# Three of nine value taps made a group ahead by ScalarE and GpSimd; key maps built 13 columns wide

## The chip, the core and the metric

The kernel runs on one core of a Trainium2 chip. The metric is the device time of one execution in microseconds (us), smaller is better.

## The reference

The program is a residual network stage of two parts on x of shape (4, 128, 96, 96) in float32. The part that matters here is the first, an attention over channels:

```
kv = einsum('oc,bchw->bohw', qkv_w, gn(x));  kv = depthwise3x3(kv, qkv_conv_w);  k, v = split(kv)
q  = idwt2(depthwise3x3 of the four bands of dwt2(gn(x)))
q, k = q / |q|, k / |k|                      (over the 96x96 pixels, 8 heads of 16 channels)
attn = softmax(q k^T * temperature);  out = proj_w @ (attn v);  x = x + out
```

The second part is two binarized 3x3 convolutions with batch norms and a residual. The change touches how `v`'s depthwise 3x3 convolution (nine taps, "value taps") is computed, and how wide the blocks are in which the matrices for `k` ("key maps") are built.

## The kernel before

The program is four blocks one after the other: `block_stats_and_projections`, `block_grams`, `block_attention`, `block_convolutions`. The change lies in `block_grams`, which I call the gram stage.

The gram stage works through NG = 32 groups of GC = 4 channels, for all four images at once. Each group is a list of J = 20 jobs, written out in `SLOTS` in four pieces:

```
"u kg mq s1 tk",  "kg s1 mq u tk",  "kg s1 mq u tk",  "kg s1 mq u mq"
```

So job 0 is a `u`, 1 `kg`, 2 `mq`, 3 `s1`, 4 `tk`, 5 `kg`, 6 `s1`, 7 `mq`, 8 `u`, 9 `tk`, 10 `kg`, 11 `s1`, 12 `mq`, 13 `u`, 14 `tk`, 15 `kg`, 16 `s1`, 17 `mq`, 18 `u`, 19 `mq`. `s1` transforms a channel's rows, `u` applies its map matrices to the result of `s1` and makes the query feature (job 8 uses job 3, 13 uses 6, 18 uses 11, and job 0 of the next group uses 16), `kg` makes the key feature, `mq` and `tk` build the map matrices of the next group in up to three blocks of MT = 7 or KT = 14 columns.

Every job goes through three engines. TensorE (PE) sums it into one of NB = 5 PSUM banks, used in turn. ScalarE (ACT) waits for the sum (`s_pe`) and copies its high half to float16 in SBUF (L839). VectorE (DVE) waits for that (`s_hi`), subtracts and stores the low half (L892), and only then is the bank free (`s_dve`): TensorE begins job n only when VectorE is done with job n - 5, and a `u` only when VectorE is done with its `s1`. All engines take their work strictly in the order of the program.

Between the jobs there is other work, at places given by tables of job numbers:

- VectorE adds the value taps 1 to 8 of the group's slab (12 image rows; SLAB = 12) in two halves, 16 instructions a group at `TAP_AT` (L885). The running sum `vsum` lies in PSUM, and the last tap of a half writes `vacc` in SBUF.
- ScalarE begins each half with a seed, tap 0 written to `vsum` (L811, at jobs 1 and 11). For the next group it normalises x (L794, four instructions, ahead of job 4) and copies its high half (L801, ahead of job 13).
- GpSimd (POOL) subtracts to get x's low half (L678), spreads taps (L687), and once in four groups computes the null parts of a head (L699 to L715).
- SyncE waits for the group's last tap, stores `vacc` (L636), then loads the slab for the group after next into the same buffer of `vin` (L616).

Once in four groups a head (16 channels) is complete. Its gram is summed by TensorE during the following four groups: pieces of ten matmuls (L975) behind the job pieces, 4 of them in the first group of the four, 3 in the second (one behind its first job piece, two behind its third and fourth), 3 in the third (two behind its first and second job piece, one behind its third), and the small null matmuls in the fourth. ScalarE copies the halves out (L821): the first in the second group, behind job 5, the second in the third group, behind job 15.

Before group 0, `lead` builds the maps of group 0 in eight jobs, and the groups 4 to 27 run in a hardware loop of three turns of eight groups.

## Time and profile before

| | |
|---|---|
| median of 3 runs (lowest, highest) | 1455.79 us (1451.62, 1458.39) |
| the profiled execution: its own time, its span | 1448.98 us, 1447.1 us |
| busy in the span: PE, DVE, ACT, POOL | 1186.5, 1087.4, 806.6, 232.0 us |
| the gram stage | from about 190 us to about 940 us of the span |
| value taps L885 in it | 448 + 64 instructions of 128x576 |

The span runs from the first to the last instruction of the profiled execution, and its own time is 1.9 us longer. The profile gives the busy time of each engine, the time at which each instruction started, what an idle engine waited for, and the clock that TensorE was granted. A VectorE or ScalarE instruction's length overlaps a little with the next one's, so the rate at which they follow each other is read from start to start.

### The profile page before, as it was taken

How to read it: one execution, taken by the hardware profiler on the slowest of the kernel's cores; microseconds unless marked ns; L12 is line 12 of the kernel's file. 1: busy time of each engine (PE TensorE's matmuls, PEld its weight loads, DVE VectorE, ACT ScalarE, POOL GpSimd, SP SyncE). 2: the span in 40 equal slices, each digit the busy share in tenths (PEclk: the TensorE clock that was granted, in tenths of full speed). 3: DMA queues.
4: the chain of work that ended last, by engine and by line, in shares of the span. 5: the costliest groups of instructions: out<-in, count | busy, mean ns of one | idle time of the engine just before them, and what ended most of it. 6: DMA issues, size and time to landing. Idle time of an engine off the chain costs nothing. (4 is left out here: it accounts for less than half of the span.)

```text
span 1447.1 us, 35967 instructions
## 1 busy us (share of the span) xinstructions
PE 1186.5 (82%) x12644; PEld 926.0 (64%) x12644; DVE 1087.4 (75%) x1899; ACT 806.6 (56%) x1414; POOL 232.0 (16%) x241
## 2 busy tenths in 40 slices
PE   0999937889899898998989999725999998999900
PEld 0555537789899898988989898603555554555500
DVE  6677428999999899998999999445767654063394
ACT  0677745667767576675667666110442443866383
POOL 6100011131131311313213221102000010000000
PEclk9999958999999899999999999867899999999955
DMA  9976962534444345444444442067877430000069
GB/s 327 419 303 267 305 144 71 138 88 123 132 100 123 108 112 137 104 115 116 108 129 116 111 127 71 22 233 240 277 254 252 134 136 0 0 1 0 1 267 401
DMA packets 148700, 221.22 MB, mean 153 GB/s; under 512 B 115624, under 2 KB 116788, under 8 KB 144192
## 3 DMA queue, kind: packets, MB, share of 16 engines
q1 hardware_dynamic: 137456, 152.26, 34.8%
q0 software_dynamic: 6480, 47.19, 8.5%
q10 hardware_dynamic: 4608, 19.67, 4.0%
q8 instruction: 101, 1.65, 0.5%
q14 instruction: 55, 0.45, 0.1%
HBM read 131.84 MB, written 87.20 MB: 151 GB/s over the span
## 5 line engine op out<-in xcount | busy, mean ns | idle before, releaser
L885 DVE SCALAR_TENSOR_TENSOR b_value_sum<-b_vin,b_vtaps,b_value_sum 128x576 f32<-128x576 f32 x448 | 361.5, 807 | 2.4 <-ACT b_value_sum L811 2.0
L1608 PE MATMUL b_conv_bank<-b_sign,wsign 128*128 (+1 forms) x1728 | 296.8, 329 | 10.3 <-ACT b_sign L1388 7.7
L1608 PEld LDWEIGHTS b_conv_bank<-b_sign,wsign 128*128 128x128 bf16 x1728 | 168.7, 98 | 141.2 <-issue 29.0
L927 PE MATMUL b_bank<-b_yh,b_tmh 96*96 96x200 f16 x768 | 198.4, 258 | 53.5 <-DVE b_feat L892 23.6
L839 ACT CAST b_feat<-b_bank 96x400 f16<-96x400 f32 x255 | 124.9, 490 | 191.4 <-PE b_bank L929 188.0
L927 PE MATMUL b_bank<-b_tkh,b_kt 96*96 96x100 f16 x1536 | 224.5, 211 | 2.5 <-DVE b_tml L908 2.3
L929 PE MATMUL b_bank<-b_tkh,b_kt 96*96 96x100 f16 x1536 | 223.5, 211 | 0.0
L928 PE MATMUL b_bank<-b_tkl,b_kt 96*96 96x100 f16 x1536 | 223.4, 211 | 0.0
L927 PEld LDWEIGHTS b_bank<-b_tkh,b_kt 96*96 96x96 f16 x1536 | 194.9, 127 | 5.0 <-DVE b_tml L908 2.5
L929 PEld LDWEIGHTS b_bank<-b_tkh,b_kt 96*96 96x96 f16 x1536 | 195.1, 127 | 0.0
L929 PE MATMUL b_bank<-b_yh,b_tml 96*96 96x200 f16 x768 | 194.2, 253 | 0.0
L928 PE MATMUL b_bank<-b_yl,b_tmh 96*96 96x200 f16 x768 | 194.2, 253 | 0.0
L928 PEld LDWEIGHTS b_bank<-b_tkl,b_kt 96*96 96x96 f16 x1536 | 193.6, 126 | 0.0
L1407 ACT CAST b_y<-b_conv_bank 128x384 f32 (+1 forms) x192 | 91.3, 478 | 172.9 <-PE b_conv_bank L1608 170.9
L678 POOL TENSOR_TENSOR b_xl<-b_xraw,b_xh 96x1536 f16<-96x1536 f32 x32 | 99.4, 3106 | 506.1 <-ACT b_xh L801 506.1
L1493 DVE BATCH_NORM_STATS2 b_bny<-b_y (+1 forms) x192 | 103.3, 554 | 100.0 <-ACT b_y L1407 99.2
L892 DVE TENSOR_TENSOR b_feat<-b_bank,b_feat 96x400 f16<-96x400 f32 x256 | 143.2, 560 | 18.7 <-ACT b_feat L839 15.6
L927 PEld LDWEIGHTS b_bank<-b_yh,b_tmh 96*96 96x96 f16 x768 | 95.2, 124 | 74.6 <-DVE b_feat L892 38.9
L461 PE MATMUL b_pk<-b_x,b_w_image 128*128 128x384 f32 x384 | 131.2, 497 | 6.8 <-DVE b_khl L362 6.7
L461 PEld LDWEIGHTS b_pk<-b_x,b_w_image 128*128 128x128 f32 x384 | 72.2, 192 | 59.7 <-DVE b_khl L362 15.3
L975 PE MATMUL b_gram<-b_feat 96*128 96x256 f16 x800 | 101.8, 277 | 2.4 <-DVE b_feat L892 1.2
L839 ACT CAST b_tmh<-b_bank 96x504 f16<-96x504 f32 (+1 forms) x155 | 99.9, 644 | 0.0
(210 smaller groups left out, 2314.2 us busy)
## 6 DMA issues: line engine op xcount, KB each, us to landing
b_vin<-value_projection_scratch SPq DMA_DIRECT2D x32, 686.0 KB, 5.5
value_projection_scratch<-b_vout ACTq DMA_DIRECT2D x24, 784.0 KB, 4.6
keys_scratch<-b_khl SPq DMA_DIRECT2D x24, 784.0 KB, 3.5
b_kt<-keys_scratch SPq DMA_DIRECT2D x128, 147.0 KB, 3.0
b_xraw<-in_x SPq DMA_DIRECT2D x128, 144.0 KB, 5.0
values_scratch<-b_vacc SPq DMA_DIRECT2D x32, 576.0 KB, 3.2
b_values<-values_scratch SPq DMA_DIRECT2D x48, 384.0 KB, 3.7
out<-xs SPq DMA_DIRECT2D x25, 576.0 KB, 6.8
```

What stands on the lines that cost most here:

```text
L461: nc.tensor.matmul(psum_k[g % NBK][:, 0:CH], w_image[:, b % 2, v, :], x[:, b, at:at + CH], start=True, stop=True).then_inc(s_mm, 1)
L678: nc.gpsimd.tensor_tensor(xh[1][:, slot, :, :, :].rearrange("h b c w -> h (b c w)"), xraw[:, slot, :], xh[0][:, slot, :, :, :].rearrange(" ...
L839: nc.scalar.copy(*target(n, 0, k)).then_inc(s_hi, 1)
L885: nc.vector.scalar_tensor_tensor(whole if t == 8 else part, src, vtaps[:, t:t + 1], part, ALU.mult, ALU.add).then_inc(s_tap, 1)
L892: nc.vector.tensor_tensor(out, src, high, ALU.subtract).then_inc(s_dve, 1)
L927: nc.tensor.matmul(out, w_hi, m_hi, start=first, stop=False)
L928: nc.tensor.matmul(out, w_hi, m_lo, start=False, stop=False)
L929: return nc.tensor.matmul(out, w_lo, m_hi, start=False, stop=last)
L975: ins = nc.tensor.matmul(gbank[:, half:half + 4 * HD * RUN], f[:, 0:2 * HD * RUN], f, start=(blk == 0), stop=(blk == S2B // RUN - 1))
L1407: nc.scalar.copy(dst, cbank[k % NBK][:, 0:CH]).then_inc(s_y, 1)
L1493: V.bn_stats(bny[:, ds(r * RC + (b * NCH + k), 1), :].rearrange("p o s -> p (o s)"), y[:, b, ds(r * (RC * CH) + k * CH, CH)]).then_inc(s_b ...
L1608: ins = nc.tensor.matmul(cbank[k % NBK][:, 0:CH].rearrange("p (r c) -> p r c", c=W), p["wsign"][nth // NIMG][:, t * C:(t + 1) * C], padded ...
```

## The change

Taps 0, 1 and 2 of a slab are no longer made in the halves. ScalarE multiplies tap 0 into `vacc` and tap 1 into the new buffer `vprod` (two instructions over the whole slab, 128x1152), a group ahead, in front of job 7 (`PRODUCTS = 7`). GpSimd adds the two, multiplies tap 2 into `vprod` and adds it (three instructions over the slab). The seed is now a copy of that sum into `vsum`, and VectorE adds the six taps 3 to 8, 12 instructions a group. On ScalarE the four instructions that normalise x stand ahead of the jobs 0, 2, 3 and 4, and x's high half ahead of job 5. The second seed moves from job 11 to job 10. `vprod` shares its memory with the buffer of the null parts, so that ScalarE waits once a head for them (`s_edge`) and GpSimd for its own sums (`s_ptap`). The key maps are built in blocks of 13 columns; there are 8 blocks as before.

```diff
-KT, KPB = 14, 3
+KT, KPB = 13, 3
...
-        eprod = sb("b2_eprod", [W, 4, 2, NIMG * HD * 2])
+        vprod = sb("b2_products", [C, SLAB * W])
+        eprod = vprod[0:W, 0:8 * NIMG * HD * 2].rearrange("p (a s n) -> p a s n", a=4, s=2)
...
-        TAP_AT = (0, 1, 2, 3, 5, 6, 7, 8, 10, 11, 12, 13, 15, 16, 17, 18)
-        SEED_AT = (1, 11)
-        NORMALISE, HIGH_X = 4, 13
+        PSTEPS = 3
+        TAPS = (3, 4, 5, 6, 7, 8)
+        NTAP = 2 * len(TAPS)
+        TAP_AT = (1, 2, 3, 4, 6, 7, 11, 12, 13, 14, 16, 17)
+        SEED_AT = (1, 10)
+        NORMALISE_AT, HIGH_X, PRODUCTS = (0, 2, 3, 4), 5, 7
...
+            def value_products(i, slot):
+                acc = vacc[:, slot, :]
+                pool.wait_ge(s_tap0, i * 2 + 2)
+                nc.gpsimd.tensor_tensor(acc, acc, vprod[:], ALU.add).then_inc(s_ptap, 1)
+                pool.wait_ge(s_ptap, i * PSTEPS + 1)
+                nc.gpsimd.tensor_tensor(vprod[:].rearrange("p (r c) -> p r c", c=W),
+                                        vin[:, slot, :].rearrange("p (r c) -> p r c", c=WP)[:, 0:SLAB, 2:2 + W],
+                                        vtaps[:, 2:3].unsqueeze(2).broadcast_to([C, SLAB, W]), ALU.mult).then_inc(s_ptap, 1)
+                pool.wait_ge(s_ptap, i * PSTEPS + 2)
+                nc.gpsimd.tensor_tensor(acc, acc, vprod[:], ALU.add).then_inc(s_ptap, 1)
...
                     low_x(i + 1, (k + 1) % 2)
+                    value_products(i + 1, (k + 1) % 2)
...
+            def products(i, slot, loads):
+                act.wait_ge(s_vin[slot], loads * 16)
+                act.wait_ge(s_vst[slot], loads * 16)
+                if not isinstance(i, int) or i:
+                    act.wait_ge(s_ptap, i * PSTEPS)
+                for t, dst in ((0, vacc[:, slot, :]), (1, vprod[:])):
+                    nc.scalar.activation(dst.rearrange("p (r c) -> p r c", c=W),
+                                         vin[:, slot, :].rearrange("p (r c) -> p r c", c=WP)[:, 0:SLAB, t:t + W],
+                                         ACT.Copy, scale=vtaps[:, t:t + 1]).then_inc(s_tap0, 1)
...
                 if half == 0:
-                    act.wait_ge(s_vin[slot], loads * 16)
+                    act.wait_ge(s_ptap, i * PSTEPS + PSTEPS)
...
-                nc.scalar.activation(vsum[:, :, 0:HALF // 2 * W].rearrange("p b (r c) -> p b r c", c=W),
-                                     src.rearrange("p (b r) c -> p b r c", b=2),
-                                     ACT.Copy, scale=vtaps[:, 0:1]).then_inc(s_seed, 1)
+                nc.scalar.copy(vsum[:, :, 0:HALF // 2 * W],
+                               vacc[:, k % 2, half * HALF * W:(half + 1) * HALF * W].rearrange("p (b n) -> p b n", b=2)).then_inc(s_seed, 1)
...
+                    if n == PRODUCTS and how != LAST:
+                        if gram is not None and k % GPH == 1:
+                            act.wait_ge(s_edge, gram + 1)
+                        products(i + 1, (k + 1) % 2, pairs + ((k + 1) // 2 + 1))
...
-            normalise(0, 0, 1)
+            for im in range(NIMG):
+                normalise(0, 0, 1, im)
             high_x(0, 0)
+            products(0, 0, 1)
```

Three places of the order in which engines take their instructions. The first is ScalarE at the start of the gram stage. Before, the eight copies of the lead jobs (`b_tkh`, `b_tmh`) follow x's high half (`b_xh`):

```order
L794 ACTIVATE b_xraw<-b_xraw,row_stats 96x384 x3
L801 CAST b_xh<-b_xraw 96x1536 [waits b2_x_normalised]
L848 CAST b_tkh<-b_bank 96x3x12x14 [waits b2_job_summed] x2
L848 CAST b_tkh<-b_bank 96x2x12x14 [waits b2_job_summed]
L848 CAST b_tmh<-b_bank 96x3x24x7 [waits b2_job_summed] x4
L848 CAST b_tmh<-b_bank 96x2x24x7 [waits b2_job_summed]
L811 ACTIVATE b_value_sum<-b_vin,b_vtaps 128x2x288 [waits b2_value_slab_in0]
```

Now the two products of slab 0, and with them the wait for its load, stand in front of the lead copies:

```order
L820 ACTIVATE b_xraw<-b_xraw,row_stats 96x384 x3
L826 CAST b_xh<-b_xraw 96x1536 [waits b2_x_normalised]
L835 ACTIVATE b_vacc<-b_vin,b_vtaps 128x1152 [waits b2_value_slab_stored0,b2_value_slab_in0]
L835 ACTIVATE b_products<-b_vin,b_vtaps 128x1152
L887 CAST b_tkh<-b_bank 96x3x12x13 [waits b2_job_summed] x2
L887 CAST b_tkh<-b_bank 96x2x12x13 [waits b2_job_summed]
L887 CAST b_tmh<-b_bank 96x3x24x7 [waits b2_job_summed] x4
```

The wait for the slab has moved from behind the lead jobs to in front of them. The second place is ScalarE in a group of the gram stage. Before, from the seed ahead of job 1 to the copy of job 7:

```order
L811 ACTIVATE b_value_sum<-b_vin,b_vtaps 128x2x288 [waits b2_value_tap_added,b2_value_slab_in1]
L839 CAST b_feat<-b_bank 96x100x4 [waits b2_job_summed]
L839 CAST b_tmh<-b_bank 96x3x24x7 [waits b2_job_summed]
L839 CAST b_yh<-b_bank 96x8x50 [waits b2_job_summed]
L794 ACTIVATE b_xraw<-b_xraw,row_stats 96x384 [waits b2_x_rows_in0]
L794 ACTIVATE b_xraw<-b_xraw,row_stats 96x384 x3
L839 CAST b_tkh<-b_bank 96x3x12x14 [waits b2_job_summed]
L839 CAST b_feat<-b_bank 96x100x4 [waits b2_job_summed]
L839 CAST b_yh<-b_bank 96x8x50 [waits b2_job_summed]
L839 CAST b_tmh<-b_bank 96x3x24x7 [waits b2_job_summed]
```

The same group after the change, from the copy of job 2 to the copy of job 7:

```order
L876 CAST b_tmh<-b_bank 96x3x24x7 [waits b2_job_summed]
L820 ACTIVATE b_xraw<-b_xraw,row_stats 96x384
L876 CAST b_yh<-b_bank 96x8x50 [waits b2_job_summed]
L820 ACTIVATE b_xraw<-b_xraw,row_stats 96x384
L876 CAST b_tkh<-b_bank 96x3x12x13 [waits b2_job_summed]
L826 CAST b_xh<-b_xraw 96x1536 [waits b2_x_normalised]
L876 CAST b_feat<-b_bank 96x100x4 [waits b2_job_summed]
L876 CAST b_yh<-b_bank 96x8x50 [waits b2_job_summed]
L835 ACTIVATE b_vacc<-b_vin,b_vtaps 128x1152 [waits b2_value_products_added,b2_value_slab_stored0,b2_value_slab_in0]
L835 ACTIVATE b_products<-b_vin,b_vtaps 128x1152
L876 CAST b_tmh<-b_bank 96x3x24x7 [waits b2_job_summed]
```

Between the copies of the jobs 1 and 7 there stand now three of the four normalising instructions, x's high half and the two products; before there were the four normalising instructions alone. The third place is VectorE from job 7 on. Before, from the low half of job 7 (`b_tml`) to that of job 11 (`b_yl`):

```order
L892 TENSOR_TENSOR b_tml<-b_bank,b_tmh 96x3x24x7
L885 SCALAR_TENSOR_TENSOR b_value_sum<-b_vin,b_vtaps,b_value_sum 128x2x288
L892 TENSOR_TENSOR b_feat<-b_bank,b_feat 96x100x4
L885 SCALAR_TENSOR_TENSOR b_vacc<-b_vin,b_vtaps,b_value_sum 128x576
L892 TENSOR_TENSOR b_tkl<-b_bank,b_tkh 96x3x12x14
L892 TENSOR_TENSOR b_feat<-b_bank,b_feat 96x100x4
L885 SCALAR_TENSOR_TENSOR b_value_sum<-b_vin,b_vtaps,b_value_sum 128x2x288
L892 TENSOR_TENSOR b_yl<-b_bank,b_yh 96x8x50
```

After the change, the same stretch:

```order
L929 TENSOR_TENSOR b_tml<-b_bank,b_tmh 96x3x24x7
L922 SCALAR_TENSOR_TENSOR b_vacc<-b_vin,b_vtaps,b_value_sum 128x576
L929 TENSOR_TENSOR b_feat<-b_bank,b_feat 96x100x4
L929 TENSOR_TENSOR b_tkl<-b_bank,b_tkh 96x3x12x13
L929 TENSOR_TENSOR b_feat<-b_bank,b_feat 96x100x4
L929 TENSOR_TENSOR b_yl<-b_bank,b_yh 96x8x50
```

The half's last tap stands behind job 7 instead of job 8, and there are no taps behind the jobs 8, 9 and 10.

## Rows read from the trace of the kernel before

**Rows 1.** Windows: busy us and (instructions) of PE, PEld, DVE, ACT, POOL; clock, DMA.

```profile
500.00:600.00 100.00, 94.92 (x1482) 89.87 (x1481) 100.00 (x167) 68.08 (x128) 27.93 (x33) 1.00 0.48 124
```

**Rows 2.** Timeline, VectorE: start us, length us, instruction; two pieces of a group.

```profile
520.27 0.50 DVE L892 TENSOR_TENSOR b_tkl<-b_bank,b_tkh 96x336 f16<-96x336 f32 x1
520.69 0.56 DVE L892 TENSOR_TENSOR b_feat<-b_bank,b_feat 96x400 f16<-96x400 f32 x1
521.17 0.81 DVE L885 SCALAR_TENSOR_TENSOR b_value_sum<-b_vin,b_vtaps,b_value_sum 128x576 f32<-128x576 f32 x1
521.89 0.57 DVE L892 TENSOR_TENSOR b_yl<-b_bank,b_yh 96x400 f16<-96x400 f32 x1
...
523.10 0.68 DVE L892 TENSOR_TENSOR b_tml<-b_bank,b_tmh 96x504 f16<-96x504 f32 x1
523.69 0.81 DVE L885 SCALAR_TENSOR_TENSOR b_value_sum<-b_vin,b_vtaps,b_value_sum 128x576 f32<-128x576 f32 x1
...
524.90 0.80 DVE L885 SCALAR_TENSOR_TENSOR b_vacc<-b_vin,b_vtaps,b_value_sum 128x576 f32<-128x576 f32 x1
```

**Rows 3.** Timeline, TensorE: first matmul of each job, start us and length us.

```profile
522.53 0.27 PE L927 MATMUL b_bank<-b_yh,b_tmh 96*96 96x200 f16 x1
...
524.12 0.21 PE L927 MATMUL b_bank<-b_tkh,b_kt 96*96 96x100 f16 x1
...
525.75 0.38 PE L937 MATMUL b_bank<-b_rm,b_map_place 126*96 126x168 f16 x3
525.97 0.21 PE L927 MATMUL b_bank<-b_ana,b_xh 96*96 96x100 f16 x1
...
526.73 1.26 PE L975 MATMUL b_gram<-b_feat 96*128 96x256 f16 x10
527.83 0.21 PE L927 MATMUL b_bank<-b_tkh,b_kt 96*96 96x100 f16 x1
```

**Rows 4.** Timeline, ScalarE: a group from its first copy, start us and length us.

```profile
524.32 0.49 ACT L839 CAST b_feat<-b_bank 96x400 f16<-96x400 f32 x1 [1.93 <-PE b_bank L929]
...
526.42 0.48 ACT L839 CAST b_feat<-b_bank 96x400 f16<-96x400 f32 x1
526.80 0.68 ACT L839 CAST b_tmh<-b_bank 96x504 f16<-96x504 f32 x1
527.34 0.50 ACT L839 CAST b_yh<-b_bank 96x400 f16<-96x400 f32 x1
527.71 2.52 ACT L794 ACTIVATE b_xraw<-b_xraw,row_stats 96x384 f32<-96x384 f32 x4
530.12 0.60 ACT L839 CAST b_tkh<-b_bank 96x504 f16<-96x504 f32 x1
...
538.21 1.46 ACT L801 CAST b_xh<-b_xraw 96x1536 f16<-96x1536 f32 x1
539.58 0.49 ACT L839 CAST b_feat<-b_bank 96x400 f16<-96x400 f32 x1
...
546.05 0.49 ACT L839 CAST b_feat<-b_bank 96x400 f16<-96x400 f32 x1 [1.93 <-PE b_bank L929]
546.44 1.07 ACT L821 COPY b_gout<-b_gram 128x512 f32<-128x512 f32 x1
```

**Rows 5.** Groups by form, ScalarE: count, busy us, mean ns; the nearest row to a product.

```profile
L1209 ACT ACTIVATE wsign<-b_w1t 128x1152 bf16<-128x1152 f32 x1 | 1.1, 1146 | 0.0
```

**Rows 6.** Tile b_xl, GpSimd: duration ns min/median/max, first and last start.

```profile
L678 POOL TENSOR_TENSOR b_xl<-b_xraw,b_xh x32: 3096/3106/3115, 202.3 to 892.8; 96x1536 f16<-96x1536 f32 x32
```

**Rows 7.** Timeline, SyncE: issue of the slab load in the same group.

```profile
526.54 0.35 SPq L616 DMA_DIRECT2D b_vin<-value_projection_scratch  x1
```

**Rows 8.** Tile b_vin: time from the issue of its loads to landing.

```profile
DMA to landing us min/median/max: 4.7/5.5/8.1
```

**Rows 9.** Timeline, ScalarE, start of the stage: idle time in brackets.

```profile
202.14 1.39 ACT L848 CAST b_tkh<-b_bank 96x504 f16<-96x504 f32 x3
...
208.25 0.74 ACT L811 ACTIVATE b_value_sum<-b_vin,b_vtaps 128x576 f32<-128x576 f32 x1 [2.12 <-DMA b_vin<-value_projection_scratch]
```

More of the change, by code:

```diff
@@ L787, in _, with normalise @@
             act.wait_ge(s_c, 7 * 16)
-            def normalise(i, slot, loads):
-                act.wait_ge(s_xin[slot], loads * LOAD)
-                for im in range(NIMG):
-                    piece = xraw[:, slot, im * GC * W:(im + 1) * GC * W]
-                    last = nc.scalar.activation(piece, piece, ACT.Identity,
-                                                bias=p["row_stats"][0:H, ds(i + (NIMG * NG + im * NG), 1)],
-                                                scale=p["row_stats"][0:H, ds(i + im * NG, 1)])
-                last.then_inc(s_xn, 1)
+            def normalise(i, slot, loads, im):
+                if im == 0:
+                    act.wait_ge(s_xin[slot], loads * LOAD)
+                piece = xraw[:, slot, im * GC * W:(im + 1) * GC * W]
+                nc.scalar.activation(piece, piece, ACT.Identity,
+                                     bias=p["row_stats"][0:H, ds(i + (NIMG * NG + im * NG), 1)],
+                                     scale=p["row_stats"][0:H, ds(i + im * NG, 1)]).then_inc(s_xn, 1)
@@ L799, in high_x @@
             def high_x(i, slot):
-                act.wait_ge(s_xn, i + 1)
+                act.wait_ge(s_xn, i * NIMG + NIMG)
                 nc.scalar.copy(xh[0][:, slot, :, :, :].rearrange("h b c w -> h (b c w)"), xraw[:, slot, :]).then_inc(s_xh, 1)
-            def seed(k, i, half, loads):
-                slot = k % 2
+            def products(i, slot, loads):
[7 more added lines that the diff above has]
+                                         ACT.Copy, scale=vtaps[:, t:t + 1]).then_inc(s_tap0, 1)
@@ L869, in _, with tap @@
             dve.wait_ge(s_c, 7 * 16)
-            def tap(k, i, m, loads):
-                slot, half, t = k % 2, m // 8, m % 8 + 1
+            def tap(k, i, m):
+                slot, half, t = k % 2, m // len(TAPS), TAPS[m % len(TAPS)]
                 src = vin[:, slot, :].rearrange("p (r c) -> p r c", c=WP)[:, half * HALF + t // 3:(half + 1) * HALF + t // 3,
@@ L900, in body @@
                     if n in TAP_AT:
-                        tap(k, i, m, pairs + (k // 2 + 1))
+                        tap(k, i, m)
                         m += 1
-                assert m == 16, m
+                assert m == NTAP, m
             for m, (kind, j) in enumerate(lead):
```

29 lines of the change are left out of this document (18 added, 11 removed).

## The prediction

> **What bounds the kernel now.** I read the windows first, for which engine has no idle time in the gram stage. VectorE is busy for all of the 100 us, TensorE for 94.92, ScalarE for 68, GpSimd for 28, at full clock [rows 1]. The timeline of VectorE then gives what each of its instructions costs from start to start: a value tap 0.72 us, a low half of 400 columns 0.48, of 504 columns 0.59, of 336 columns 0.42 [rows 2]. A group has 16 taps, 12 low halves of 400 columns, six of 504 (four `mq`, two `tk`) and two of 336: 11.5 + 5.8 + 3.5 + 0.8 = 21.7 us. The first copies of two successive groups on ScalarE are 546.05 - 524.32 = 21.73 us apart [rows 4]. So a group takes just what VectorE needs, and VectorE is the bound.
>
> How far behind is TensorE? Its timeline gives a `u` 1.59 us, a `kg` 1.63, a build of three blocks 0.22, an `s1` 0.54, ten gram matmuls 1.10 [rows 3]. Four `u`, four `kg`, four `s1` and the 22 blocks are 6.4 + 6.5 + 2.2 + 1.6 = 16.7 us. With 4, 3, 3 and 0 gram pieces a group needs 21.1, 20.0, 20.0 and about 17.4 us (a bit under 1 us for the null matmuls, an estimate). TensorE alone would thus allow 19.6 us a group on average.
>
> **VectorE after the change.** Four taps fewer save 2.9 us. The `tk` halves shrink by 36 columns in 504, at 0.59 - 0.42 = 0.17 us for 168 columns 0.04 us each. VectorE then needs 18.7 to 18.8 us a group. If only totals counted, a group would take max(21.1, 18.8), 20.0, 20.0, 18.8, a mean of 20.0, and 32 groups would save some 55 us.
>
> **But ScalarE stands in the middle of each job.** A copy that comes late delays VectorE, and VectorE holds the bank of job n until TensorE wants it for job n + 5. So I walk through one group, from T, where ScalarE starts the copy of job 0. That is the end of TensorE's `u` (0.20 us past the start of the next job). Job 1, a `kg`, ends at T + 1.63 [rows 3, 4]. From there ScalarE has without a gap, in its new order: copy `kg` 0.38, normalise 0.60 (2.41 for four), copy `mq` 0.54, normalise 0.60, copy `s1` 0.37, normalise 0.60, copy `tk` 0.44 (0.60 long, less the overlap and the narrower block), x's high half 1.37, two copies 0.76, the products, and the copy of job 7 with its full length 0.68 [rows 4].
>
> A product is new. Its form is that of the old seed, 0.74 us for 576 elements [rows 9]. Between x's high half (1536 columns, 1.46) and a copy of 400 columns (0.49) an element costs 0.86 ns [rows 4], so 576 more make 1.24 us long, 1.17 from start to start. The lower bound is the row of 1152 elements without the scale from memory, 1146 ns [rows 5], about 1.07 from start to start; the upper one is twice a seed, 1.48 [rows 9]. I take 1.17, since form and length both lie between rows. The Trainium skill (ScalarE: Activation LUTs, section "What ACT_TABLE_LOAD costs") gives 280 ns + 0.833 ns an element for an ACTIVATE with one operand by pointer, an estimate of 1240 ns. By rows 5 alone each group's chain would be 0.2 us shorter.
>
> The sum is 6.34 without the two products and 8.68 with them: the copy of job 7 ends at T + 10.31. VectorE, idle by then, does low half 7 (0.59), the tap behind it (0.72), low half 8 (0.56 long): T + 12.2 with the handover. Only now may TensorE start job 13, which it could have reached at about T + 11.4 with two gram pieces in the way, and at T + 10.3 with one. Behind it in TensorE's queue are `u` 1.59, two blocks 0.15, `kg` 1.63, `s1` 0.54, three blocks 0.22, `u` 1.59, two blocks 0.15, the gram pieces of 1.10 each, and the next group's job 0, 1.59 + 0.20. That is 7.66 us and two, one or no gram pieces. On VectorE the low halves and taps from job 7 to job 16 take 9.1 us from T + 10.3, with 0.3 us in it for the seed at job 10, which must wait for the tap behind job 7; job 0 of the next group needs low half 16, so T' is not before 10.3 + 9.1 + 1.8 = T + 21.2. The four groups of a head give:
>
> - first (two pieces in the second half): 12.3 + 7.66 + 2.2 = 22.1 us;
> - second: the gram copy of 1.07 us [rows 4] stands ahead of job 7 too, so 23.1 to 23.2;
> - third: one piece, 21.0, so VectorE's 21.2;
> - fourth: 21.2.
>
> Together 87.7 us, where before there are 4 x 21.74 = 87.0. **The relief of VectorE is thus handed to ScalarE's order**: six full heads cost 6 x 0.7 = 4 us. The groups 0 to 3 have no gram pieces: 0.5 us saved each, 2 us. The last group has nothing to normalise or to multiply: it saves about 2 us of the 2.9. The first three of the last head together cost 1 us. At the four ends of a straight or looped stretch TensorE is done earlier by 0.5 us: 2 us saved. Sum of the stage: +4 - 2 - 2 + 1 - 2 = -1 us.
>
> **The start.** Before, the lead copies start at 202.14, and ScalarE waits for slab 0 only behind them, until 208.25 [rows 9]. Now slab 0's wait and its two products stand ahead: the lead copies start at 208.2 + 2.35 = 210.6, 8.4 us later. Queued behind are all lead copies, on VectorE their low halves, and TensorE's job 1. GpSimd's part of slab 0 hides in this: three times 1152 elements, 3.106 us for 1536 [rows 6] make 2.33 us each, done 7.4 us after the products at 218.0, while job 1's sum is ready at about 219. So +8.4 us, with 0.3 for the seed 8.7.
>
> **What else is costed at nothing.** GpSimd's 7.4 us a group lie between T + 9.6 and T + 17.1, and the seed wants them at T' + 0.4, so 4 us of cover; with the null parts (2304 elements, an estimate of 6 us from rows 6) it is done about 1.5 us into the next group, ahead of x's high half at 6.5 and the `s_edge` wait at 8. If GpSimd took over 11 us, the seed and all copies behind it would wait. The Trainium skill (GPSIMD Engine Reference, "8. Key points") says that GpSimd's SBUF interfaces are shared with VectorE, and that VectorE instructions with two SBUF inputs or in a two-port mode contend. The trace shows GpSimd at 3096 to 3115 ns in all 32 cases beside a full VectorE [rows 6]; VectorE's inputs there are one in PSUM and one in SBUF.
>
> The slab has less cover. Its load is issued after the last tap, 0.84 us behind that tap's end (524.90 + 0.80, then 526.54) [rows 2, 7], and lands 5.5 us later, at worst 8.1 [rows 8]. The last tap now ends 0.2 us after T' in a short group, so the slab is there at T' + 6.5, and the products want it at T' + 7.3.
>
> **Sum.** -1 + 8.7 = +7.7 us on the profiled execution's 1448.98, so 1456.7. That execution lies 6.8 us below the median of 1455.79; on the median I get 1463.5 us.
>
> **Rivals.**
>
> - *The relief arrives* (faster). If ScalarE's chain is no bound, for instance because its pieces run closer together than I add them, a group goes to 20.0 us: 1.7 x 28 = 48 us and 5 at the ends, less 8.7: 1411 us. For it: TensorE and VectorE have the totals. Against: each term of the chain is a row of the same instruction, and the chain would have to be 2 us shorter. Half a microsecond less in each group gives 14 us, 1449. The sign turns where the chain is 0.3 us shorter than my 8.68. 20% for all of this side beyond the half per cent.
> - *The slab comes late* (slower). If a load takes 8.1 us as the slowest did, the products wait 1.8 us at T' + 7.3, and everything behind them too: 28 groups, +50, 1513 us; if a third of the loads do, 1480. It decides from a landing time of 6.3 us on. 12%.
> - *VectorE and GpSimd slow each other.* GpSimd's busy time per group grows by 7.4 us; if a tenth of it were lost on either engine, 0.7 us a group or 22 in all, 1485. The unchanged 3106 ns speak against it, and by the skill's rule nothing contends. 3%.
> - *The start costs nothing*, if the slab lands earlier: 1455. The load is issued by the same queue at the same place, so 5%.
> - *My forecast*, chain-bound groups of 21.6 to 22.3 us on average: 1455 to 1475, 60%.
>
> **From these the chances.** The products' bounds move the chain by -0.2 to +0.6 us, 6 us down and 18 up over the stage. This measurement tells about half a per cent, 7.3 us, from no change, and my forecast lies just at this edge: slower by more than that 0.47, within it 0.32, faster 0.21. The range for eight times in ten goes from 1436, most of the way to the half-microsecond rival and beyond, to 1484.
>
> **What would show each step.** In the changed kernel's profile VectorE should have 12 taps a group and be idle some 2 us before low half 7, waiting for ScalarE; a product should be 1.24 us long; TensorE should wait for VectorE's `feat` low half ahead of job 13; successive groups should be 22.1, 23.2, 21.2, 21.2 us; the lead copies should start near 210.6, behind a wait for the slab's DMA. I am wrong if TensorE's waits in the stage shrink to nothing (then the first rival), or if the products wait for the slab in most groups (the second).

## The result, and the profile after

| | before | after |
|---|---|---|
| median of 11 runs (lowest, highest), us | 1455.79 (1447.56, 1458.39) | 1462.15 (1459.49, 1469.23) |
| the profiled execution: time, span, us | 1448.98, 1447.1 | 1467.67, 1466.0 |
| T of group 4, T of group 28, start of the last tap, us | 301.86, 833.77, 918.5 | 307.03, 852.21, 936.7 |

The ratio after/before is 1.0065, 95% interval 1.0043 to 1.0088: a little slower. The two profiled executions lie at the edges of their runs, one 6.8 us below its median and one 5.5 us above. They differ by 18.7 us where the medians differ by 6.4. So I read from the traces which terms there are, and from the medians how large the sum is.

The page of the changed kernel begins with the span and the busy times:

```profile
span 1466.0 us, 36146 instructions
...
PE 1190.4 (81%) x12644; PEld 939.5 (64%) x12644; DVE 1001.6 (68%) x1771; ACT 871.2 (59%) x1478; POOL 467.6 (32%) x337
```

VectorE has lost 86 us of work, and the kernel did not become faster. The timeline of ScalarE in the group that begins at T = 514.18, from its first copy to the copy of job 8 (the rows that answer to [rows 4]):

```profile
514.18 0.49 ACT L876 CAST b_feat<-b_bank 96x400 f16<-96x400 f32 x1 [1.34 <-PE b_bank L966]
...
515.81 0.49 ACT L876 CAST b_feat<-b_bank 96x400 f16<-96x400 f32 x1 [0.60 <-PE b_bank L966]
...
519.37 1.47 ACT L826 CAST b_xh<-b_xraw 96x1536 f16<-96x1536 f32 x1
520.74 0.49 ACT L876 CAST b_feat<-b_bank 96x400 f16<-96x400 f32 x1
521.12 0.50 ACT L876 CAST b_yh<-b_bank 96x400 f16<-96x400 f32 x1
521.51 1.27 ACT L835 ACTIVATE b_vacc<-b_vin,b_vtaps 128x1152 f32<-128x1152 f32 x1
522.66 1.25 ACT L835 ACTIVATE b_products<-b_vin,b_vtaps 128x1152 f32<-128x1152 f32 x1
523.81 0.67 ACT L876 CAST b_tmh<-b_bank 96x504 f16<-96x504 f32 x1
524.35 0.49 ACT L876 CAST b_feat<-b_bank 96x400 f16<-96x400 f32 x1
```

From 515.81 on there is no idle time in brackets: ScalarE has the chain of the prediction, and the copy of job 7 ends at 523.81 + 0.67 = 524.48, T + 10.30 (predicted T + 10.31). VectorE in the same group:

```profile
524.51 0.69 DVE L929 TENSOR_TENSOR b_tml<-b_bank,b_tmh 96x504 f16<-96x504 f32 x1 [1.40 <-ACT b_tmh L876]
525.11 0.80 DVE L922 SCALAR_TENSOR_TENSOR b_vacc<-b_vin,b_vtaps,b_value_sum 128x576 f32<-128x576 f32 x1
525.83 0.56 DVE L929 TENSOR_TENSOR b_feat<-b_bank,b_feat 96x400 f16<-96x400 f32 x1
...
528.35 0.57 DVE L929 TENSOR_TENSOR b_yl<-b_bank,b_yh 96x400 f16<-96x400 f32 x1 [0.74 <-ACT b_yh L876]
```

VectorE, which before was never idle [rows 1], waits 1.40 us ahead of low half 7, and low half 8 is done at 525.83 + 0.56 = T + 12.21, as walked. The 0.74 ahead of low half 11 is ScalarE's gram copy, of which more below. TensorE pays, as the list of waits from 160 to 960 us shows (engine, what it wanted, who had it, us in total, times, longest):

```profile
DVE b_feat L929 <- ACT b_feat L876: 61.4, 56, 4.1
DVE b_tml L929 <- ACT b_tmh L876: 45.3, 31, 3.0
...
PE b_bank L964 <- DVE b_feat L929: 34.2, 43, 2.7
...
PE b_bank L974 <- DVE b_tml L929: 12.9, 19, 1.5
```

Four groups of a head and, last, the first group of another head, in windows from T to T (the columns of [rows 1]):

```profile
558.17:579.93 21.76, 19.75 (x323) 19.12 (x321) 18.49 (x32) 17.38 (x31) 11.36 (x6) 0.92 0.43 115
579.93:603.64 23.71, 22.05 (x321) 21.13 (x319) 19.88 (x34) 16.44 (x30) 15.75 (x13) 0.93 0.44 120
603.64:625.55 21.91, 20.39 (x321) 19.52 (x319) 18.11 (x30) 17.22 (x30) 12.80 (x9) 1.00 0.41 109
625.55:647.62 22.07, 21.29 (x331) 20.57 (x329) 19.97 (x35) 16.45 (x29) 11.36 (x6) 1.00 0.43 115
764.70:786.78 22.08, 20.41 (x321) 19.61 (x319) 19.59 (x34) 16.44 (x30) 14.38 (x12) 1.00 0.45 122
```

They are a fourth, a first, a second and a third group of four. At full clock a first group takes 22.08. But of the five first groups 4, 8, 16, 24 and 28 (12 and 20 begin a later turn of the loop) four took 23.7 at a clock of 0.93, and of the fourth groups 7, 15, 23 and 27 (11 and 19 end a turn) three ran below 1.00, at 0.85 and 0.92. The third groups, where TensorE has only one of the two waits shown next, 0.78, ran at 1.00, but for group 22, whose slab came late. Before, all these groups took 21.74 to 21.82 at 1.00. That loss of clock stands nowhere in my prediction. The two rows of TensorE's timeline that answer for it, in the first group of 23.71 us and then in that of 22.08:

```profile
591.00 0.42 PE L974 MATMUL b_bank<-b_rm,b_map_place 126*96 126x168 f16 x3 [0.54 <-DVE b_tml L929]
592.21 0.29 PE L964 MATMUL b_bank<-b_yh,b_tmh 96*96 96x200 f16 x1 [0.78 <-DVE b_feat L929]
595.04 0.47 PE L974 MATMUL b_bank<-b_rk,b_key_place 117*96 117x156 f16 x2
...
775.77 0.42 PE L974 MATMUL b_bank<-b_rm,b_map_place 126*96 126x168 f16 x3 [0.54 <-DVE b_tml L929]
776.98 0.29 PE L964 MATMUL b_bank<-b_yh,b_tmh 96*96 96x200 f16 x1 [0.78 <-DVE b_feat L929]
778.58 0.30 PE L974 MATMUL b_bank<-b_rk,b_key_place 117*96 117x156 f16 x2
```

The waits are the same, 0.54 ahead of job 12 and 0.78 ahead of job 13, at the same places. Behind them `u` 13 takes 595.04 - 592.21 = 2.83 us in one and 778.58 - 776.98 = 1.60 in the other. The windows there show the clock (the third is the slow stretch of the first group by itself):

```profile
590.00:595.00 5.00, 3.68 (x32) 3.37 (x30) 4.64 (x8) 3.10 (x7) 4.64 (x3) 0.74 0.15 34
774.00:779.00 5.00, 3.67 (x54) 3.34 (x52) 3.87 (x7) 4.08 (x9) 4.75 (x3) 1.00 0.13 35
592.40:595.80 3.40, 3.40 (x23) 3.28 (x22) 3.31 (x6) 1.85 (x5) 3.04 (x3) 0.51 0.01 2
```

TensorE runs at 1.2 GHz instead of 2.4 for about 3.4 us, from just behind the second wait (the window of 5 us ends inside that stretch). So waits of 1.3 us in all may be followed by another loss of 1.6 us, and whether they are isn't settled by the waits alone.

At the start of the stage ScalarE's timeline shows (answering to [rows 9]):

```profile
208.16 1.25 ACT L835 ACTIVATE b_vacc<-b_vin,b_vtaps 128x1152 f32<-128x1152 f32 x1 [5.92 <-DMA b_vin<-value_projection_scratch]
209.33 1.24 ACT L835 ACTIVATE b_products<-b_vin,b_vtaps 128x1152 f32<-128x1152 f32 x1
210.47 1.35 ACT L887 CAST b_tkh<-b_bank 96x468 f16<-96x468 f32 x3
...
218.49 0.64 ACT L845 COPY b_value_sum<-b_vacc 128x576 f32<-128x576 f32 x1 [3.51 <-POOL b_vacc L736]
219.07 0.48 ACT L876 CAST b_feat<-b_bank 96x400 f16<-96x400 f32 x1
```

The lead copies start at 210.47 (predicted 210.6) and the first copy of a job is 8.4 us later than before (219.07, before 210.64). The seed in front of it waits 3.51 us for GpSimd, which I had taken as hidden. Nearly all of that wait costs nothing: the first copy needs TensorE's first `kg` as well, whose last matmul starts at 218.50 and is 0.29 us long, so without the seed it would have come only some 0.3 us earlier.

### The profile page after: what moved, and what is told of

Its sections match the earlier page's. It is cut to its first block and busy times, and to the rows that moved or that the text cites. A ratio compares the mean times of both kernels' runs of the same rounds, so it can differ in the third digit from the quotient of the medians.

```text
span 1466.0 us, 36146 instructions
## 1 busy us (share of the span) xinstructions
PE 1190.4 (81%) x12644; PEld 939.5 (64%) x12644; DVE 1001.6 (68%) x1771; ACT 871.2 (59%) x1478; POOL 467.6 (32%) x337
## 5 line engine op out<-in xcount | busy, mean ns | idle before, releaser
L922 DVE SCALAR_TENSOR_TENSOR b_value_sum<-b_vin,b_vtaps,b_value_sum 128x576 f32<-128x576 f32 x320 | 258.1, 807 | 0.1
L964 PE MATMUL b_bank<-b_tkh,b_kt 96*96 96x100 f16 x1536 | 229.4, 214 | 4.2 <-DVE b_tml L945 2.2
L965 PE MATMUL b_bank<-b_tkl,b_kt 96*96 96x100 f16 x1536 | 228.6, 213 | 0.0
L966 PE MATMUL b_bank<-b_tkh,b_kt 96*96 96x100 f16 x1536 | 228.3, 213 | 0.0
L964 PEld LDWEIGHTS b_bank<-b_tkh,b_kt 96*96 96x96 f16 x1536 | 198.9, 130 | 6.1 <-DVE b_feat L929 2.7
L966 PEld LDWEIGHTS b_bank<-b_tkh,b_kt 96*96 96x96 f16 x1536 | 198.5, 129 | 0.0
L966 PE MATMUL b_bank<-b_yh,b_tml 96*96 96x200 f16 x768 | 198.3, 258 | 0.0
L965 PE MATMUL b_bank<-b_yl,b_tmh 96*96 96x200 f16 x768 | 197.7, 257 | 0.0
L965 PEld LDWEIGHTS b_bank<-b_tkl,b_kt 96*96 96x96 f16 x1536 | 197.3, 128 | 0.0
L929 DVE TENSOR_TENSOR b_tml<-b_bank,b_tmh 96x504 f16<-96x504 f32 (+1 forms) x155 | 99.1, 640 | 45.3 <-ACT b_tmh L876 45.3
L1012 PE MATMUL b_gram<-b_feat 96*128 96x256 f16 x800 | 104.8, 282 | 2.4 <-DVE b_feat L929 1.2
```

The source lines that it names most:

```text
L922: nc.vector.scalar_tensor_tensor(whole if t == TAPS[-1] else part, src, vtaps[:, t:t + 1], part, ALU.mult, ALU.add).then_inc(s_tap, 1)
L929: nc.vector.tensor_tensor(out, src, high, ALU.subtract).then_inc(s_dve, 1)
L964: nc.tensor.matmul(out, w_hi, m_hi, start=first, stop=False)
L965: nc.tensor.matmul(out, w_hi, m_lo, start=False, stop=False)
L966: return nc.tensor.matmul(out, w_lo, m_hi, start=False, stop=last)
L1012: ins = nc.tensor.matmul(gbank[:, half:half + 4 * HD * RUN], f[:, 0:2 * HD * RUN], f, start=(blk == 0), stop=(blk == S2B // RUN - 1))
```

## The experiments

Each kernel was run beside the kernel before on the same chip, and the median of that one moves between 1449.9 and 1455.8 us from chip to chip. So the ratios are compared (1% is 14.5 us). "Group" is the mean of a first, second, third and fourth group in the profiled execution that ran at a clock of 1.00 (with GpSimd's steps of one row no fourth group did, and one of 21.8 us at 0.92 is taken). My theory is the chain: ScalarE's work between the copies of the jobs 1 and 8 sets the length of a group. The rivals are a total or a contention between engines.

| kernel | median us | ratio to before | interval | group, us |
|---|---|---|---|---|
| after | 1462.15 | 1.0065 | 1.0043, 1.0088 | 21.9 |
| products ahead of job 8 | 1431.75 | 0.9857 | 0.9827, 0.9888 | 21.0 |
| products ahead of job 9 | 1428.06 | 0.9831 | 0.9787, 0.9875 | 20.8 |
| x's high half at job 13 | 1429.42 | 0.9850 | 0.9802, 0.9898 | 20.6 |
| products of one row | 1416.39 | 0.9740 | 0.9700, 0.9781 | 20.5 |
| GpSimd's steps of one row | 1463.64 | 1.0086 | 1.0055, 1.0117 | 22.0 |
| TensorE repeats in its waits | 1465.28 | 1.0103 | 1.0063, 1.0142 | 21.9 |
| first gram copy at job 15 | 1460.53 | 1.0060 | 1.0037, 1.0083 | 21.7 |
| slab 0 loaded first | 1460.76 | 1.0083 | 1.0053, 1.0114 | 21.9 |
| products at 9, slab 0 first | 1424.24 | 0.9819 | 0.9780, 0.9857 | 20.8 |
| the same, sum of slab 0 early | 1422.14 | 0.9789 | 0.9758, 0.9820 | 20.8 |
| the same, gram copy at 15 | 1413.23 | 0.9734 | 0.9704, 0.9764 | 20.6 |
| before, 13 columns only | 1453.20 | 1.0003 | 0.9971, 1.0035 | 21.6 |

### Where the products stand

```diff
-        NORMALISE_AT, HIGH_X, PRODUCTS = (0, 2, 3, 4), 5, 7
+        NORMALISE_AT, HIGH_X, PRODUCTS = (0, 2, 3, 4), 5, 9
```

> The two products stand ahead of job 9 instead of job 7 on ScalarE; nothing else is changed. Chain theory: the copies of the jobs 7 and 8 come 2.4 us earlier, VectorE's low half of job 8 is done at about T + 9.8, and TensorE starts job 13 without a wait. The gap that TensorE has ahead of job 13 and the one ahead of job 12 go, the granted clock of all groups returns to 1.00, and groups come to 20.0 to 21.1 us, 20.4 on average, where they are 21.8 to 23.7 now. That is 1405 to 1420 us against 1462. Rival (VectorE and GpSimd or the DMA slow each other, or a total and not an order is the bound): the work on each engine is the same, so groups stay at 22 us on average and the time within 5 us of 1462. Slab rival: the products are wanted later by 2 us, so if the slab's landing were what holds the groups, this would help too, but then the wait of ScalarE for the slab would have to be seen in most groups of the changed kernel, and it is seen in three of 32.

Measured: 1428.06, a ratio of 0.9831 where the change has 1.0065, so 2.3% or 34 us from one number. The time came out above the expected 1420. The windows say why (a fourth, a first, a second and a third group):

```profile
541.86:562.52 20.66, 18.55 (x323) 17.52 (x321) 18.54 (x32) 17.13 (x31) 11.31 (x6) 1.00 0.46 123
562.52:583.10 20.58, 20.21 (x321) 19.52 (x319) 19.23 (x34) 16.19 (x29) 12.13 (x8) 1.00 0.47 130
583.10:604.31 21.21, 20.22 (x321) 19.52 (x319) 18.89 (x32) 17.20 (x31) 16.44 (x15) 1.00 0.44 119
604.31:625.22 20.91, 20.91 (x331) 20.49 (x329) 19.55 (x34) 16.19 (x30) 11.33 (x6) 1.00 0.46 121
```

The clock is 1.00 in all four, and the third group has TensorE busy for all of its 20.91 us: TensorE is the bound there. The mean of 20.8 is 0.4 above the expected 20.4, from what still stands in the order of the others (the gram copy in the second, waits for VectorE's `b_yl` in the fourth). The work on each engine is that of the changed kernel, so no engine's total and no contention made its 22 us.

The same edit with 8 in place of 9 is the finer question, since job 13 waits for low half 8:

> The two products one job later than in the changed kernel, ahead of job 8 on ScalarE. Chain theory in its exact form: the copy of job 7 then ends at T + 8.0 and that of job 8 at T + 10.8, low half 8 is done at T + 11.4 instead of T + 12.2. The wait of TensorE ahead of job 12 goes, the one ahead of job 13 stays in part (0.5 us in the first group of the four, under 0.3 us in the others). Groups of 21.3, 21.2, 21.3 and 21.0 us, so about halfway between the changed kernel and the one with the products at job 9: 1432 to 1442 us. If what matters were only that the products leave the first seven jobs, or some contention in that stretch, it would do as much as job 9: 1428.

Measured: groups of 21.12, 21.20, 21.11 and 20.67 us where 21.3, 21.2, 21.3 and 21.0 were expected, and 1431.75 us, 0.3 us below the range. The time is not halfway, as I had expected: most of the 34 us is already there, and by the intervals (0.9857 and 0.9831) the times alone don't tell job 8 from job 9. The trace does. TensorE's waits in the first group of the four, ahead of job 8 and ahead of job 13:

```profile
568.06 0.29 PE L964 MATMUL b_bank<-b_yh,b_tmh 96*96 96x200 f16 x1 [0.34 <-DVE b_yl L929]
574.08 0.29 PE L964 MATMUL b_bank<-b_yh,b_tmh 96*96 96x200 f16 x1 [0.56 <-DVE b_feat L929]
```

The wait ahead of job 8 (for the result of its `s1`) is in the changed kernel too. The one ahead of job 12 is gone, and the one ahead of job 13 is 0.56 us (expected 0.5); with the products at job 9 it is gone as well, and a first group takes 20.58 in place of 21.12. I take the chain as shown. Part of the 34 us is the clock, which in this trace and in that of job 9 stays at 1.00 in all groups from 2 to 30 but those where a turn ends or begins.

### The chain made shorter in other ways

x's high half goes back to job 13, and GpSimd makes the sum of the products ahead of x's low half:

```diff
-        NORMALISE_AT, HIGH_X, PRODUCTS = (0, 2, 3, 4), 5, 7
+        NORMALISE_AT, HIGH_X, PRODUCTS = (0, 2, 3, 4), 13, 7
...
-                    low_x(i + 1, (k + 1) % 2)
                     value_products(i + 1, (k + 1) % 2)
+                    low_x(i + 1, (k + 1) % 2)
```

> x's high half goes back from job 5 to job 13 on ScalarE, as in the kernel before; the products stay ahead of job 7; GpSimd makes the sum of the products before x's low half. Chain theory: ScalarE's chain from job 1 to job 7 is 1.37 us shorter, so 7.3 us, and the wait of TensorE ahead of job 13 shrinks from 1.4 us to nothing or 0.2 us: groups of 20.3 to 21.1 us, 1416 to 1430 us. But the products are then wanted at T + 5.9 us, while a slab lands 5.7 to 6.5 us after T: waits of up to 0.6 us for the slab may take some of it back, up to 15 us over the stage. Contention theory: the same instructions on all engines, so no change from 1462, within 5 us.

Measured: 1429.42 us, at the upper end. The feared waits for the slab are there behind the start:

```profile
ACT b_vacc L835 <- DMA b_vin<-value_projection_scratch: 7.4, 8, 1.8
```

Eight products wait, 7.4 us in total, and the group of the longest wait, 1.82 us, took 25.78. In the kernel with the products at job 9 none of the 31 slabs behind the first was late. This is the second rival of the prediction come true in part: it needs the products 1.4 us earlier than the change has them.

The third way leaves the order and takes the work out (the new argument is the number of rows that each product is made over):

```diff
-                        products(i + 1, (k + 1) % 2, pairs + ((k + 1) // 2 + 1))
+                        products(i + 1, (k + 1) % 2, pairs + ((k + 1) // 2 + 1), SLAB if k == 0 else 1)
```

> From the third group on ScalarE multiplies only one of the twelve rows of each product, 96 elements for 1152, so the value sums of those groups are left unmade in eleven rows. It takes 0.9 us off each product, 1.8 us a group, and nothing off GpSimd or VectorE. Chain theory: the copy of job 7 ends at T + 8.5 instead of T + 10.3 and the wait ahead of job 13 goes with it: groups of 20.1 to 21.1 us, 1410 to 1425 us. Rival, that ScalarE's order is no bound and the time is lost between VectorE and GpSimd: under 5 us from 1462.

Measured: 1416.39, inside the range; groups of 19.90, 20.58, 20.43 and 20.91 us. A change that takes 1.8 us of ScalarE's work a group saves 1.4 us a group, although ScalarE was idle for about 5 us of each 22 (17.22 of 21.91 busy in the window above).

### GpSimd's part

```diff
-                nc.gpsimd.tensor_tensor(acc, acc, vprod[:], ALU.add).then_inc(s_ptap, 1)
+                nc.gpsimd.tensor_tensor(acc[:, 0:W], acc[:, 0:W], vprod[:, 0:W], ALU.add).then_inc(s_ptap, 1)
```

and the same for the other two steps.

> GpSimd's three steps of a slab's sum (add, multiply, add) work over one of twelve rows, so the sums of eleven rows are left incomplete. GpSimd's busy time falls by about 6.5 us a group, ScalarE and VectorE keep every instruction. Chain theory: GpSimd's sum is covered, so nothing changes: within 4 us of 1462. Contention theory (a tenth of GpSimd's added time is lost on VectorE): taps of VectorE become shorter than 807 ns and groups 0.7 us shorter, 1440 us.

Measured: 1463.64; the interval of its ratio overlaps that of the changed kernel, so no change is shown. The taps by form, first in this kernel, then in the changed one:

```profile
L922 DVE SCALAR_TENSOR_TENSOR b_value_sum<-b_vin,b_vtaps,b_value_sum 128x576 f32<-128x576 f32 x320 | 258.8, 809 | 0.1
...
L922 DVE SCALAR_TENSOR_TENSOR b_value_sum<-b_vin,b_vtaps,b_value_sum 128x576 f32<-128x576 f32 x320 | 258.1, 807 | 0.1
```

GpSimd's busy time falls from 467.6 to 268.3 us and a tap takes 809 ns instead of 807. So GpSimd's steps do not lengthen the taps of this form. The Trainium skill (GPSIMD Engine Reference, section "8. Key points") names instructions with two inputs in SBUF or in a two-port mode as those that contend; a tap has its running sum in PSUM, so the trace agrees.

### The clock

In the first and the fourth group of each four, TensorE repeats work in its waits:

```diff
-                            build(kind, c, bank[n % NB], (k + 1) % 2)
+                            build(kind, c, bank[n % NB], (k + 1) % 2, 4 if gram is not None and n == 12 and k % GPH in (0, 3) else 1)
...
-                            run(n, k)
+                            run(n, k, 2 if gram is not None and n == 11 and k % GPH in (0, 3) else 1)
```

> In the first and the fourth group of each four, TensorE makes its s1 of job 11 twice over and its blocks of job 12 four times over, with the same result in the same bank. That is 0.54 us of matmuls in front of a wait of 0.54 to 0.60 us and 0.66 us in front of one of 0.78 us, so TensorE is busy where it waited and nothing is later. Clock theory: the first group of the four takes 23.7 us instead of 22.1 in six of seven cases because TensorE's short waits let the granted clock fall from 2.4 to 1.2 GHz for some 3 us; with the waits filled it stays, those groups take 22.1 us, and 7 to 12 us go: 1450 to 1455 us. If the clock has another cause, the groups stay at 23.7 us and the time at 1462; if the added matmuls cost what they last, 1462 to 1475.

Measured: 1465.28 where 1450 to 1455 was expected, so nothing won. It lies in the range that I had named for repeats that cost what they last, but the groups say otherwise. The windows of a fourth and a first group, and of one group without repeats:

```profile
558.55:579.93 21.38, 19.66 (x344) 18.76 (x342) 18.10 (x31) 17.39 (x31) 11.37 (x6) 1.00 0.44 119
579.93:602.01 22.08, 21.61 (x342) 20.80 (x340) 19.97 (x35) 16.45 (x29) 14.36 (x12) 1.00 0.45 122
804.17:830.37 26.20, 24.51 (x331) 23.32 (x329) 20.32 (x35) 16.56 (x30) 11.34 (x6) 0.87 0.39 103
```

At the place of the edit the clock theory holds: from group 4 on, all nine first and fourth groups that do not begin or end a turn of the loop ran at 1.00, in 22.08 and 21.4 us, so the repeats cost nothing there; in the four traces where such waits are not filled (the changed kernel, GpSimd's steps of one row, first gram copy at job 15, slab 0 loaded first) 15 of 36 did. From group 4 to group 28 this execution is 6.2 us shorter than the changed kernel's. But groups that the edit does not touch were slower in this execution: 24.29 and 22.89 us for the groups 1 and 3 (22.15 and 21.47 in the changed kernel), so that group 4 began 5.8 us later, and 26.20 for one whose slab came 0.81 us late:

```profile
812.43 1.26 ACT L835 ACTIVATE b_vacc<-b_vin,b_vtaps 128x1152 f32<-128x1152 f32 x1 [0.81 <-DMA b_vin<-value_projection_scratch]
```

Its sisters take 22.07, so the group with a wait of 0.81 us on ScalarE was 4.1 us longer, and most of that goes with the lower clock: 0.50 from 820 to 824 us. In group 18 of the same execution ScalarE waited 1.01 us for its slab; the clock stayed at 1.00 and the group took 23.18, only 1.1 more. The kernel with GpSimd's steps of one row speaks against a large price without being meant to: it has the same waits of 0.53 and 0.78 us, and four of its five first groups kept the clock (22.07), where in the changed kernel one did; their medians are the same. So it is shown that the clock falls behind such waits in some groups and not in others, and that with the waits filled it stayed up in all nine. For the executions that weren't profiled there is the mean granted clock of the whole program: 0.915 to 0.924 in the eleven of the changed kernel (median 0.920), 0.921 to 0.925 in the five with repeats (median 0.923), and medians of 0.9265 to 0.9295 for the kernel before on the three chips of these experiments. The clock thus rose part of the way and the time did not fall; what the repeats or the early groups cost in its place stays open.

### The gram copy

```diff
-        START, COPY_AT, NULL_AT = [0, 6], [5, 11, 14], 12
+        START, COPY_AT, NULL_AT = [0, 6], [6, 11, 14], 12
```

> The first gram copy of a head (1.07 us on ScalarE, in the second group of the four) moves from behind job 10 to behind job 15; nothing else differs from the changed kernel. Corrected walk: this copy delays the copy of job 11 and with it VectorE by 0.7 us in the second group, whose 21.9 us are 21.2 plus this; it becomes 21.2, in seven groups: 5 us less, 1457 us. If the second group is held by TensorE and its gram pieces alone, as I had walked it before the change was run, it stays at 21.9 and the time at 1462.

Measured: the second group takes 21.10 us in place of 21.91 to 21.93 in the trace, as the corrected walk has it. In the time it shows as 1.0060 against 1.0065, with intervals of a quarter of a per cent: 5 us are not excluded and not shown. In company with the products at job 9 (below) the same edit takes the second group from 21.20 to 20.37, and there the ratio falls from 0.9789 to 0.9734, with intervals that just overlap.

### The start

```diff
-            for i in range(2):
-                load_rows(xraw, d["x_rows"], s_xin, i, i)
-                load_keys(i, i)
-            for i in range(2):
-                load_slab(i * SLAB * WP, i)
+            load_slab(0, 0)
+            load_rows(xraw, d["x_rows"], s_xin, 0, 0)
+            load_keys(0, 0)
+            load_rows(xraw, d["x_rows"], s_xin, 1, 1)
+            load_keys(1, 1)
+            load_slab(SLAB * WP, 1)
```

> SyncE loads slab 0 ahead of the rows and keys of groups 0 and 1 instead of behind them; nothing else differs from the changed kernel. Start theory: the 8.4 us that the start lost are ScalarE's wait for slab 0 (5.9 us) and the two products (2.4 us) in front of the lead copies. The wait goes, the lead copies start at about 204.5 instead of 210.5, and all behind them is 5.5 to 6 us earlier: 1456 us. The rows of x land later by the slab's share, so up to 1 us of it may go again. Rival (the start costs nothing, since the stage waits for something else there): the last tap ends at the same time, 1462 us.

Measured: 1460.76 where 1456 was expected, and a ratio of 1.0083, so no gain in the time; in the trace the last tap ends 2.5 us earlier, not 5.5 to 6. The lead copies start at 206.53, with no wait in front of the products, but:

```profile
216.03 0.64 ACT L846 COPY b_value_sum<-b_vacc 128x576 f32<-128x576 f32 x1 [5.00 <-POOL b_vacc L737]
```

The first seed now waits 5.00 us for GpSimd. Both products and lead copies were about 4 us earlier, and what came last was the other branch: products, x's low half and the tap spreading on GpSimd, three steps of the sum, seed.

> Both edits together: the products ahead of job 9 and slab 0 loaded first. They act at different places, the start and the groups, so their gains should add: 1428 for the products ahead of job 9, less 5.5 to 6, so 1422 us. If the slab's wait at the start were covered by the first groups, it would be 1428.

Measured: 1424.24 and 0.9819, against 0.9831 without the slab edit: 2 us, less than the intervals resolve and in line with what the trace shows for the edit alone. Then the products of slab 0 go ahead of the normalising, and GpSimd's sum ahead of x's low half:

```diff
+            products(0, 0, 1)
             for im in range(NIMG):
                 normalise(0, 0, 1, im)
             high_x(0, 0)
-            products(0, 0, 1)
...
+            value_products(0, 0)
             low_x(0, 0)
             spread_taps(1, 1)
-            value_products(0, 0)
```

> The kernel with the products ahead of job 9 and slab 0 loaded first, and now also the products of slab 0 ahead of the normalising of group 0 on ScalarE, and GpSimd's sum of slab 0 ahead of x's low half. Theory of the start: with slab 0 loaded first, the first seed waited 5.0 us for GpSimd's sum, which ended at 216.0. Here the products run at 199 to 201 us, the sum ends at 208.5 to 209, the lead copies start at 205, the first copy of a job at 210 instead of 216.6: 6 to 7 us less than 1424, so 1418 us. If the first groups had been held by TensorE's slow clock there and not by the seed, less than 2 us.

Measured: 1422.14 where 1418 was expected. ScalarE's timeline:

```profile
205.08 1.37 ACT L888 CAST b_tkh<-b_bank 96x468 f16<-96x468 f32 x3
...
209.45 0.68 ACT L846 COPY b_value_sum<-b_vacc 128x576 f32<-128x576 f32 x1
213.45 0.49 ACT L877 CAST b_feat<-b_bank 96x400 f16<-96x400 f32 x1 [3.31 <-PE b_bank L967]
```

The seed waits for nobody, and the first copy comes 2.9 us earlier than with the slab loaded first, not 6 to 7. Now TensorE is last: its first `kg` begins at 210.18, behind VectorE's last lead low half, and takes 3.0 us at the low clock of the start. Three branches (the lead jobs and TensorE, the slab's wait, GpSimd's sum) were within a few microseconds of each other, so each edit gives only the distance to the next one.

> The same with the first gram copy of a head behind job 15. The second group of the four takes 21.2 us with the products at job 9, of which 0.6 us come from the copy ahead of job 11 (the other groups take 20.6 to 20.9): 0.4 to 0.6 us in seven groups, 3 to 4 us less than the kernel without it, so 1414 us.

Measured: 1413.23, ratio 0.9734: 2.7% below the kernel before and 3.3% below the changed kernel. That it meets the expected 1414 is luck: the kernel without the edit had come out 4 us above its forecast, and the edit gave 8.9 us in the medians where 3 to 4 were expected. The trace shows 0.84 us less in each second group but the last (0.40), 5.4 us in all seven. Its windows (a first, a second and a third group, and a fourth from another head):

```profile
551.77:572.35 20.58, 20.21 (x321) 19.53 (x319) 19.22 (x34) 16.19 (x29) 12.13 (x8) 1.00 0.47 130
572.35:592.72 20.37, 20.01 (x321) 19.44 (x319) 18.80 (x32) 17.00 (x31) 16.43 (x15) 1.00 0.46 124
592.72:613.63 20.91, 20.91 (x331) 20.48 (x329) 19.56 (x34) 16.18 (x30) 11.34 (x6) 1.00 0.45 121
700.58:721.23 20.65, 18.56 (x323) 17.52 (x321) 18.54 (x32) 17.13 (x31) 11.32 (x6) 1.00 0.46 123
```

### The width of the key maps

```diff
-KT, KPB = 14, 3
+KT, KPB = 13, 3
```

in the kernel before.

> The kernel before with key maps built in blocks of 13 columns instead of 14, the smallest part of the change by itself. 36 columns less in each of two low halves and copies a group: 0.09 us a group off VectorE, which bounds every group there, so 2 to 3 us less than the kernel before, a ratio of 0.998 to 1.000. If VectorE were not the bound, nothing.

Measured: a ratio of 1.0003, interval 0.9971 to 1.0035, too wide for an edit of 0.2%. In the trace a group takes 21.63 us where it took 21.74, so the edit acts as it should: VectorE was the bound, and 0.11 us of it go.

## Why the prediction was right, and where it was not

- **VectorE's relief is handed to ScalarE's order**: right, and shown by three edits that shorten the same chain in different ways. Its terms came within 0.02 us: a product 1.15 from start to start in the rows above (1.17), the copy of job 7 at T + 10.30 (10.31), low half 8 at T + 12.21 (12.2).
- **The groups of a head**: 22.1, 23.1 to 23.2, 21.2 and 21.2 predicted, a sum of 87.7; 22.08, 21.92, 22.07 and 21.4 to 21.8 measured, a sum of 87.5 to 87.8. The sum is right by luck, its parts are not. I had read `chunk(k, n)` one piece too low, in the description of the kernel as well: the first group has three gram pieces (behind its second, third and fourth job piece), the second has three (behind its first, second and fourth), the third has four. The first gram copy stands behind job 10 of the second group, the second behind job 0 of the fourth. With these places the same walk, made after the result, gives what was measured: two pieces behind job 13 in the first and third group, 12.21 + 7.66 + 2.2 = 22.07; in the second VectorE's 21.2 plus its idle 0.74 for the gram copy, 21.9.
- **The clock**: missing. I costed TensorE's waits at their length. In the profiled execution the groups 4, 7, 8 and 16 took 1.6 us more each, and group 22, with a slab 1.47 us late, 3.2 more: 9.7 us of the 13.3 by which the groups 4 to 27 together were longer than before, where I had put 4 us, less 1 to 2 at the ends of the turns. The medians hold this loss too: the granted clock of the whole program has a median of 0.920 in the changed kernel's eleven executions, against 0.919 in the profiled one. The longer executions are mostly those with the lower clock; the kernel before took 1458.96 and 1460.17 us in two at 0.919, and 1452.1 to 1453.8 in five at 0.925. At nearly the same clock as the fastest execution of the changed kernel (1459.49 at 0.924) it took 1453.4 and 1457.9. So some 5 us are left at equal clock, an estimate from these times that compares kernels run on different chips, and the rest of the 9.5 us in the ratio goes with the lower clock.
- **The start**: 8.4 us as walked up to the first copy of a job, though the branch that came last was GpSimd's and not TensorE's, by some 0.3 us. I had the GpSimd sum hidden (done at 218.0, the sum of job 1 ready at 219); it was done at 218.4, ScalarE was ready for the seed at 215.0, and job 1 was summed at about 218.8. By group 4 the loss is 5.2 us (predicted 8.7 - 2).
- **GpSimd beside VectorE, the narrower key maps, the slab**: as predicted; the steps of the sum take 2632, 2107 and 2632 ns (7.4 us a group predicted, 7.7 with the gaps between them measured), and two slabs behind the first were late, by 0.22 and 1.47 us. The prediction's 7.4 us was not what its own row gives: three times 2.33 are 7.0. The two additions took 0.3 us more each than that row scaled, the multiplication 0.2 less.
- **The number**: 1463.5 predicted, 1462.15 measured. The sum of +7.7 us stands against +6.4 in the medians and 0.65%, or 9.5 us, in the ratio. That it came so close is luck in part: a loss of clock that I had at nothing was met by errors the other way. One of them is that I set the result of a walk against the profiled execution of before, a fast one at a clock of 0.929, and carried its 6.8 us to the median over unchanged, which the changed kernel need not keep: its own profiled execution lies 5.5 us above the median. Which errors make up the rest stays open.
- **The first rival** (the relief arrives) did not come about, but its place is where the two numbers 7 and 9 differ: 34 us. That the sign turned on the order of two instructions is what the chances said, with 0.21 for faster.

## What to carry to other kernels

When work moves from the busiest engine to one that stands in the middle of every job, walk one period in the order of that engine's queue, from a copy to the copy on which a later engine waits; an engine that is idle for a fifth of each group can set the pace. Try the long instructions at a place where no engine is yet waiting for the copy behind them; here that was two jobs later and worth 2.3% of the whole. Where a stage start has several branches of nearly equal length, price an edit by the distance to the second branch, not by the wait that it removes. Where TensorE's waits are new, look at the granted clock behind them: here a wait could cost more than its length.
